# Second attention of a two-layer transformer kernel: q and k turned once and stacked by transfers, the output's two parts summed as they leave PSUM

## The reference, cut to what matters

```python
qkv = jnp.einsum('bld,ed->ble', x, w_qkv).reshape(B, L, 3, H, D).transpose(2, 0, 3, 1, 4)   # H = 16, D = 16
q, k, v = rmsnorm(qkv[0], q_norm_w), rmsnorm(qkv[1], k_norm_w), qkv[2]
attn = softmax(jnp.einsum('bhqd,bhkd->bhqk', q, k) * D ** -0.5, axis=-1)
out = jnp.einsum('bhqk,bhkd->bqhd', attn, v).reshape(B, L, dim)
out = jnp.einsum('bld,ed->ble', out, w_proj) + b_proj
# beside it, on the same normalised x: 8 routed experts (top 2) of 176 and a shared one of 352, SwiGLU
```

## Time and profile before

| | |
|---|---|
| time before, median of 3 | 1409.52 us (1408.64 to 1409.75) |
| the profiled execution | 1408.91 us, its span 1407.1 us |
| granted TensorE clock, mean | 0.998 |
| second layer's slots | from 889 us on, first scores at 918.7, last at 1383.9 |

### The profile page before, as it was taken

How to read it: one execution, slowest core, us unless ns; L and a number is a source line. 1 busy time by engine, 2 the same in 40 slices (tenths; PEclk the granted TensorE clock), 3 DMA queues, 4 the chain that set the end, 5 groups by cost and what they waited for, 6 DMA issues and landing times. The chain is left out here.

```text
span 1407.1 us, 25856 instructions
## 1 busy us (share of the span) xinstructions
PE 1368.9 (97%) x8950; PEld 1221.1 (87%) x8950; DVE 920.9 (65%) x1793; ACT 820.0 (58%) x2172; POOL 761.9 (54%) x757
## 2 busy tenths in 40 slices
PE   9999899999999999999999999899999999999997
PEld 7887798999899989998999888788889888889887
DVE  6655566565656565656665665677777878777764
ACT  5553444554544555445544544378787788778873
POOL 2651433454434454435544443477669677777764
PEclk9999999999999999999999999999999999999999
DMA  5995333334332343223433334144233242342442
GB/s 197 323 330 198 85 91 89 92 80 120 100 94 52 101 130 99 75 75 98 114 86 94 113 75 165 68 122 150 83 98 123 68 150 84 120 120 92 143 122 90
DMA packets 85681, 165.64 MB, mean 118 GB/s; under 512 B 16720, under 2 KB 27664, under 8 KB 83248
## 3 DMA queue, kind: packets, MB, share of 16 engines
q1 hardware_dynamic: 85552, 163.99, 38.3%
HBM read 99.90 MB, written 22.09 MB: 87 GB/s over the span
## 5 line engine op out<-in xcount | busy, mean ns | idle before, releaser
L775 POOL TENSOR_TENSOR a_pr<-a_pr,a_ri 128x512 f32<-128x512 f32 x128 | 133.5, 1043 | 299.1 <-DVE a_ri L955 299.1
L832 ACT ACTIVATE a_pr<-a_score,a_nb 128x256 f32<-128x256 f32 x256 | 119.3, 471 | 266.3 <-DVE a_nb L947 266.3
L1337 POOL TENSOR_TENSOR l_pr<-l_pr,l_ri 128x512 f32<-128x512 f32 x128 | 133.5, 1043 | 119.0 <-DVE l_ri L1714 118.1
L1465 ACT ACTIVATE l_pr<-l_score,l_nb 128x256 f32<-128x256 f32 x256 | 119.2, 472 | 80.8 <-DVE l_nb L1680 80.2
L58 PE MATMUL a_job<-s_xs,s_wh 128*128 128x512 f32 x384 | 153.9, 401 | 1.0 <-PEq L221 1.0
L60 PE MATMUL a_job<-s_xs,s_wl 128*128 128x512 f32 x384 | 151.7, 395 | 0.0
L59 PE MATMUL a_job<-s_xs,s_wh 128*128 128x512 f32 x384 | 151.3, 394 | 0.0
L947 DVE TENSOR_REDUCE a_nb<-a_score 128x2 f32<-128x512 f32 x128 | 88.5, 692 | 85.0 <-PE a_score L1026 83.3
L1680 DVE TENSOR_REDUCE l_nb<-l_score 128x2 f32<-128x512 f32 x128 | 87.5, 684 | 34.0 <-PE l_score L1820 33.4
L960 DVE TENSOR_TENSOR a_pt<-a_turn,a_pt 128x512 fp32r<-128x512 f32 x128 | 87.5, 683 | 24.2 <-ACT a_pt L840 24.2
L1844 PE MATMUL l_out<-s_wh,l_vp 128*128 128x256 f32 x512 | 91.6, 300 | 0.9 <-DVE s_wh L1684 0.9
(11 more groups left out here) (257 smaller groups left out, 4780.3 us busy)
## 6 DMA issues: line engine op xcount, KB each, us to landing
s_wl<-wgu_scratch SPq DMA_DIRECT2D x56, 512.0 KB, 4.8
a_sk<-a_rotk SPq DMA_DIRECT2D x384, 64.0 KB, 2.0
a_sq<-a_rotq SPq DMA_DIRECT2D x256, 64.0 KB, 2.0
s_xs<-xn_scratch SPq DMA_DIRECT2D x14, 1024.0 KB, 5.6
l_wd<-wd_scratch SPq DMA_DIRECT2D x56, 256.0 KB, 2.7
a_raw<-in_w SPq DMA_DIRECT2D x30, 256.0 KB, 3.0
wgu_scratch<-f_split SPq DMA_DIRECT2D x14, 512.0 KB, 4.7
f_praw<-in_moe_w SPq DMA_DIRECT2D x14, 384.0 KB, 4.5
```

The costliest lines, as they stand in the source:

```text
L775: pool.tensor_tensor(e, e, ri[:, n % 2, :].unsqueeze(2).broadcast_to([P, 2, SEQ]), ALU.mult)\
L832: i = act.activation(pr[:, n % 2, t, :], PS[n % 2][:, t * SEQ:(t + 1) * SEQ], ACT.Exp, bias=nb[:, n % 2, t:t + 1], accum_out=sm[:, n % 2, ...
L1337: pool.tensor_tensor(e, e, ri[:, n % 3, :].unsqueeze(2).broadcast_to([P, 2, SEQ]), ALU.mult)\
L1465: i = act.activation(pr[:, n % 3, t, :], PS[n % NPS][:, t * SEQ:(t + 1) * SEQ], ACT.Exp, bias=nb[:, n % 3, t:t + 1], accum_out=sm[:, n % 3 ...
```

## The change

The columns of w_qkv for q and k are ordered by the host so that a transpose of 128 columns gives rows (head in a pair group, dimension, pair). For each half of the heads one job X turns q and k once (four transposes for both), ScalarE copies the high and VectorE subtracts for the low part. SyncE stores the four pieces in DRAM and loads them back as stacks, two pairs of heads at once, each row as often as the stack needs it: 8 stores and 12 loads a batch. Stacks have 4 slots instead of 3. Sum of squares and scaling follow the new order of columns (the 16 elements of a head are 4 words apart). The values' low parts go to rows 64 to 127 of the output bank; ScalarE copies one half of it across, VectorE adds the other, and two groups of four heads make one tile of 128 rows, which is split and projected: P0 and P1 have 6 matmuls each. w_proj is one piece instead of two. The planner has new goals (28.1 and 18), and SyncE's list gets the transfers of a slot ahead of the tile weights that open after it.

```diff
-VG, VSTRIDE, VBLK = 4, 160, 640
+VG, VB, VSTRIDE, VBLK = 4, 2, 144, 576
+VHALF = VG * D1
...
-    NJ, NPS, NSTK, NGU, ND, NCB, NHID = 3, 1, 3, 3, 3, 3, 3
+    NJ, NPS, NSTK, NGU, ND, NCB, NHID = 3, 1, 4, 3, 3, 3, 3
+    PER_LOAD = 2
...
-    UNIT, SLOT_GOAL, EARLY_GOAL = 10, 30.6, 14
+    UNIT, SLOT_GOAL, EARLY_GOAL = 10, 28.1, 18
+
+    def X_AT(m):
+        return (8, 9) if m == 0 else (8, 10)
...
-        m, r = divmod(n + 4, H1)
-        if r % 2 == 0 and 0 <= m < BATCH:
-            jobs.append((f"S{r // 2}", m))
+        if b + 1 < BATCH and u in X_AT(b + 1):
+            jobs.append((f"X{X_AT(b + 1).index(u)}", b + 1))
...
+    OPENS = [AT["D1", K - 1 - ND] if K > ND else AT["U", K] - 2 for K in range(L + 1)]
+    STACK_AT = [[n for n in SLOTS if (OPENS[K - 1] if K else SLOTS[0] - 1) < n <= (OPENS[K] if K < L else SLOTS[-1])] for K in range(L + 1)]
...
+                def store_stack(m, half):
+                    wait_free(sp, (f"X{half}", m))
+                    for low in range(2):
+                        sp.dma_start(qs_dram[m % 2, half, :, :, low].rearrange("h d p n -> (h d) p n"), tqk[:, half, 0, low, :].bitcast(F32))                           .then_inc(tqk_out[half], 16)
+                        sp.dma_start(ks_dram[m % 2, half, :, low].rearrange("h d p n -> h (d p) n"), tqk[:, half, 1, low, :].bitcast(F32))                           .then_inc(tqk_out[half], 16)
+
+                def load_stack(i):
+                    pair = i * PER_LOAD
+                    m, p = divmod(pair, H1 // 2)
+                    at = slice(pair % NSTK, pair % NSTK + PER_LOAD)
+                    if p % 4 == 0:
+                        sp.wait_ge(tqk_out[p // 4], 16 * 4 * (m + 1))
+                    if pair >= NSTK:
+                        sp.wait_ge(S["score_full"], 2 * (pair + PER_LOAD - NSTK))
+                    half, j = divmod(p, 4)
+                    for h in range(2):
+                        own = qs_dram[m % 2, half, h, :, :, j:j + PER_LOAD].rearrange("d c p n -> (d c) (p n)")
+                        sp.dma_start(zq[64 * h:64 * h + 64, h, at, :].bitcast(F32).rearrange("r p n -> r (p n)"),
+                                      own.unsqueeze(0).broadcast_to([2, 2 * D1, PER_LOAD * SEQ])).then_inc(zq_in[stack_of(i)], 16)
+                    own = ks_dram[m % 2, half, :, :, :, j:j + PER_LOAD].rearrange("h c d p n -> (h c d) (p n)")
+                    sp.dma_start(sk[:, at, :].bitcast(F32).rearrange("r p n -> r (p n)"),
+                                  own.unsqueeze(1).broadcast_to([4 * D1, 2, PER_LOAD * SEQ])).then_inc(sk_in[stack_of(i)], 16)
+
+                def transfers(n):
+                    m, u = n // H1 + 1, n % H1
+                    if m < BATCH and u - 1 in X_AT(m):
+                        store_stack(m, X_AT(m).index(u - 1))
+                    if n % (2 * PER_LOAD) == 0 and 0 <= n // (2 * PER_LOAD) + 1 < N // (2 * PER_LOAD):
+                        load_stack(n // (2 * PER_LOAD) + 1)
...
                 for K in range(L + 1):
+                    for n in STACK_AT[K]:
+                        transfers(n)
                     if 2 <= K < L:
                         load_gu(K)
...
+                def out_low(g):
+                    here, there = VHALF * (g % 2), VHALF * (1 - g % 2)
                     act.wait_ge(S["pv_done"], 4 * g + 4)
-                    if g >= VG:
-                        wait_full(act, ("P1", g // VG - 1))
-                    act.activation(ot[:, 0, g % VG, :], PO[:, 0:SEQ], ACT.Copy).then_inc(S["out_hi"], 1)
+                    act.activation(ol[here:here + VHALF, :], PO[there:there + VHALF, 0:SEQ], ACT.Copy).then_inc(S["out_low"], 1)
+
+                def out_hi(k):
+                    act.wait_ge(S["out_free"], 2 * k + 2)
+                    if k >= VB:
+                        wait_full(act, ("P1", k // VB - 1))
+                    act.activation(ot[:, 0, k % VB, :], os[:, k % VB, :], ACT.Copy).then_inc(S["out_hi"], 1)
...
-                    own(dve.tensor_reduce(ss[:, :], sqr[:, :, :].rearrange("p t (g d) -> p (t g) d", d=D1), AX.X, ALU.add))
+                    own(dve.tensor_reduce(ss[:, :].rearrange("p (g q) -> p g q", q=4), sqr[:, :, :].rearrange("p t (g d q) -> p (t g) q d", d=D1, q=4), AX.X, ALU.add))
...
+                def out_sum(g):
+                    here = VHALF * (g % 2)
+                    dve.wait_ge(S["out_low"], g + 1)
+                    if g >= 4:
+                        dve.wait_ge(S["out_lo"], (g - 4) // 2 + 1)
+                    dve.tensor_tensor(os[here:here + VHALF, g // 2 % VB, :], PO[here:here + VHALF, 0:SEQ], ol[here:here + VHALF, :], ALU.add)\
+                       .then_inc(S["out_free"], 1)
+
+                def out_lo(k):
+                    dve.wait_ge(S["out_hi"], k + 1)
+                    dve.tensor_tensor(ot[:, 1, k % VB, :], os[:, k % VB, :], ot[:, 0, k % VB, :], ALU.subtract).then_inc(S["out_lo"], 1)
...
+                    if n >= 10 and (n - 10) % 8 == 0 and (n - 10) // 8 < VB * BATCH:
+                        out_lo((n - 10) // 8)
                     for item in second:
                         job_out(item)
...
+                    elif name[0] == "X":
+                        half = int(name[1])
+                        pe.wait_ge(S["weighted"], m + 1)
+                        for part in range(2):
                             for t in range(TB):
+                                at = part * D + half * P
+                                i = pe.transpose(bank[:, part * SEQ + t * P:part * SEQ + (t + 1) * P], qk[:, t, at:at + P], ident[:, :])
...
-                    if u % 2 == 0:
-                        wait_free(pe, (f"S{u // 2}", m))
+                    if u % (2 * PER_LOAD) == 0:
+                        i = n // (2 * PER_LOAD)
+                        pe.wait_ge(zq_in[stack_of(i)], 16 * 2 * (n // (2 * NSTK) + 1))
+                        pe.wait_ge(sk_in[stack_of(i)], 16 * (n // (2 * NSTK) + 1))
```

## The result

The changed kernel takes 1502.95 us (median of 4 runs, 1499.57 to 1504.22) against 1409.41 of the kernel before on the same chip: ratio 1.0661, 95% interval 1.0642 to 1.0679. The forecast was 1390, range 1375 to 1403: wrong in size and in sign. The profiled span is 1497.8 us.

What follows compares the result with a forecast made beforehand. TensorE was taken to set the pace, with 14.9 us of the middle lost to other engines. Middle -29.0, early part +10.6 and tail -1.3 summed to -19.7 us: forecast 1390, range 1375 to 1403.

Steps and rivals of the forecast that it cites:

- So I cost them at nothing in the middle, hidden by three slots: Second layer's middle: stack loads, issued three slots (9.8 us) before their scores, cost nothing.
- Rival (c): Stack loads land late, at 32 x the lateness; 0.6 us at each would take the 19.7 us gain; chance 0.08.
- A TensorE instruction taken out is worth its units: Middle: TensorE sets the pace at 0.116 us a unit, so 318 units fewer give 36.9 us less.
- (b): VectorE becomes the bound: 1398 if the reduction alone doubles, 1407 if the scaling does too; chance 0.12.
- Sum of squares taken at no change: VectorE, slots 2: the strided sum stays at 1.208 us, with up to twice the time (8.4 us more) kept for the range.
- P0's wait on the low part: Slot 3: the projection waits for the output's last low part, 0.6 us a batch over 7 batches.
- X0's wait on the weighted q: Slot 8: the transpose for the stacks waits for the weighted q, 0 to 1.5 us, taken as 0.6 a batch.
- VectorE's exchange: Middle: VectorE loses four k_lo, 3.0 us a batch, and gains subtractions and half-height adds, about 2: no gain there.
- ScalarE's term of -2: Middle: ScalarE loses copies, so slots of the shared experts get easier, 2 us off the loss.
- The early part: Before the second layer's first scores: +10.6 us, with a 5.1 us stall for tile 3's weights and 5.6 of moved work.
- The clock term of 1.5: Early part: after an idle of 5 us TensorE's lower clock comes once more, +1.5 us, bounds 0 and 3.
- The tail: After the last scores: 18 units fewer give 2.1 us, later projection waits add 0.8, so -1.3 us.

Runs made afterwards that it cites:

- both edits: The changed kernel with each z_q load and each k store split in two, 32 issues a batch instead of 20: 1429.65 us, ratio 1.0155.

## Why the prediction was wrong

**The step that failed first: "So I cost them at nothing in the middle, hidden by three slots".** Landing was taken from loads of another shape: 4.8 us for 512 KB. It measured 9.0 for the k stack and 9.6 for the weights, since two of the new forms run at about 50 GB/s and hold up the rest. TensorE waits 34.6 us for the k stack, 22.3 for weights, and GpSimd 39.8 for combine rows, all priced at nothing. Splitting the two forms is worth 58.9 us in the middle and 10.2 ahead of it, 73.3 in all. Rival (c) had the direction right, stack loads that land late, and not the size: at the median the k stack lands after 9.0 us, inside the 9.8 of cover, so its price of "32 x lateness" would have given nothing. It was 9 loads of 32, late by up to 9.8 us, and the rival had no term for weights and combine rows. It got 0.08, on the ground that the DMA share was 0.38. A mean share over all engines says nothing of two of them. The rule that speaks against the change stood on a page that was cited for something else.

**The step that failed second: "A TensorE instruction taken out is worth its units".** The middle's gain of 29.0 us rested on 318 units at 0.116. Slots with 28 units do run in 3.25 us where little else is to be done (the last sixteen take 3.21 to 3.35 in each kernel with all transfers over 16 engines that leaves P and X in their slots), so the unit was right. But TensorE's units alone, taken out of the kernel before, give a third and a fifth of their time. With transfers repaired the time is 39.9 over the forecast, and the middle, at 469.7, is 33.5 over its 436.2. The nearest rival is (b), VectorE as the bound, at 0.12, with too small a price: I let it act in the slots of the strided sum, and TensorE's waits on VectorE come to 31.3 us of the middle, 15.7 of them at the turn. The kernel with both edits has its excess in slots 1 to 3 (22 us over eight batches), 7 and 8 (14), 11 (5), 13 and 14 (12). That it is VectorE in each of them isn't shown: 11.2 us of TensorE's waits end otherwise, and four stretches of lower clock cost something too. Moving VectorE's copies of slots 0 and 1 to ScalarE gives back 4.8 of the middle, all of it in slots 1 to 3 (17.8 to 12.9).

**The terms on the loss.** Sum of squares taken at no change: 1.21 to 2.01 us, worth 3.0 us of time by the medians, not clear of noise; the bound of twice the time held. P0's wait on the low part, 0.6 us a batch: 7 waits, 10.8 us, 1.5 each. X0's wait on the weighted q, 0.6: 2.7 us in 4 places in the change, 5.0 in 5 with transfers repaired, 1.0 each. The sum of separate waits was the wrong form for both: removing them brought nothing. VectorE's exchange, "about 2" us gained for four k_lo lost, was right in sum: two subtractions of 0.69, and four half-height adds of 0.42 for two subtractions of 0.41 fewer, 2.2 in all. An add over 64 rows takes 0.417 us, about as much as a subtraction over 128 (0.406). ScalarE's term of -2 had nothing to win: TensorE waited for ScalarE 0.4 us in the whole middle before.

**The early part, forecast 929.3, measured 944.6.** The structure was right, a stall for tile 3's weights behind the stores, its size not. The waits of TensorE:

```profile
909.45 0.66 PE L1790 MATMUL l_job<-s_ident,l_qk 128*128 128x128 f32 x4 [2.03 <-DVE l_ga L1609]
929.28 0.77 PE L59 MATMUL l_job<-l_xs,s_wl 128*128 128x512 f32 x1 [13.71 <-DMA s_wl<-wgu_scratch]
944.59 0.77 PE L1838 MATMUL l_score<-l_sk,l_zq 128*128 128x256 f32 x2 [5.41 <-DMA l_sk<-ks_scratch]
```

and SyncE's issues, first and last of eight stores and then the weights:

```profile
912.25 0.56 SPq L1271 DMA_DIRECT2D qs_scratch<-l_tqk  x1
...
919.38 0.50 SPq L1272 DMA_DIRECT2D ks_scratch<-l_tqk  x1
919.93 2.82 SPq L1245 DMA_DIRECT2D s_wl<-wgu_scratch  x1
```

The stall was forecast at 5.1 with bounds 2 and 8. I had four issues of 0.4 behind X1, reckoned from the shortest one, 0.32; all eight stand behind 912.25, at 0.50 to 2.95 each, and the weights need 9.3 us, where 4.8 was taken. With both edits the stall is 7.8 and the first scores come at 934.4. I also left out the first stacks: they are loaded behind the combine rows' way through DRAM, 5.4 us late. The clock term of 1.5 was nothing on balance: the lower level that stood at 900 to 904 before is gone, and TensorE works at it from 929.3 to 932 instead. The landing of 3.2 us that the prediction gives beside its sum comes from a fit that the Trainium skill states for transfers issued by GpSimd; SyncE issues these, and it entered no sum.

**The tail**, forecast at 21.9, takes 24.9. At a clock of 0.88 against 0.96 before, TensorE is busy 15.0 us of it, where it was 16.0 with 18 units more; the rest is waiting.

## What to carry to other kernels

Before transfers are called hidden, read off each new one its slowest dimension on both sides; here a leading broadcast and a leading head index of 2 left the DMA share at 0.14 and doubled the landing of the transfers behind them. A busy share of 97% does not make an engine's time worth its time: take its instructions alone out of the kernel, as one run, before building the change that is to save them. Then ask which engine ends the waits that take its place. And where a planner places the work, a change of its goals is a change by itself, here of 8 us: test it alone, and count which stage the work moves to.

## What the runs showed of the hardware

With z_q loads on their way, and in the second window k stores too (128 KB each, a slowest dimension of 2), 52 and 48 GB/s move at a DMA share of 0.14, and the issue of the next two z_q loads takes SyncE 2.9 and 1.3 us. Split in two, the parts land 2.1 (k) and 2.6 us (z_q) after issue; with the 2 moved behind a dimension of 32, the whole load of 128 KB lands after 3.4. An issue takes SyncE 0.51 us for a z_q load, 0.52 for a k store and 0.58 for a q store, against 0.43 for the weights (medians; the shortest for weights is 0.32).

After 3.6 us of idle that end at 1068.75, TensorE is busy throughout the window from 1069.0 to 1072.5, at a granted clock of 0.56: nearly all of it at 1.2 GHz. The kernel with both edits has four such stretches in its middle (granted 0.52 from 1009.3 to 1012.7, 0.51 from 1050.3 to 1053.7), the kernel before none. At half the clock each costs, as an estimate, about half of its 3.4 us.
